# Recurrent part of a graph network: tile sums in two PSUM banks, a third of the second half's n gate computed ahead, last half's gates in PSUM

## The reference, cut to what matters

```python
def step(h, _):
    messages = h[col] @ W_msg.T + b_msg
    agg = jax.ops.segment_sum(messages, row, num_segments=num_nodes)   # 50000 nodes; row is src, col is dst
    gi = agg @ W_ih.T + b_ih
    gh = h @ W_hh.T + b_hh
    r = sigmoid(i_r + h_r);  z = sigmoid(i_z + h_z)
    n = tanh(i_n + r * h_n)
    return (1 - z) * n + z * h
```

## Time and profile before

| | |
|---|---|
| median of 3 runs | 5896.12 us |
| the profiled execution's own time | 5895.16 us |
| its span in the trace | 5893.1 us |
| PE busy | 3913.6 us (66%) |
| DVE busy | 3931.6 us (67%) |
| POOL busy | 3402.2 us (58%) |
| ACT busy | 2444.6 us (41%) |
| mean granted TensorE clock | 0.835 |
| tile sums, first L1678 to last L1783 start, steps 0 to 4 | 3081.2 to 3334.5, 3644.5 to 3899.1, 4211.7 to 4466.3, 4779.6 to 5035.1, 5349.1 to 5592.6 us |

### The profile page before, as it was taken

How to read it: one execution, slowest core, us unless ns; L and a number is a source line. 1 busy time by engine, 2 the same in 40 slices (tenths; PEclk the granted TensorE clock), 3 DMA queues, 4 the chain that set the end, 5 groups by cost and what they waited for, 6 DMA issues and landing times. The chain is left out here.

```text
span 5893.1 us, 58110 instructions
## 1 busy us (share of the span) xinstructions
PE 3913.6 (66%) x14140; PEld 2165.5 (37%) x14140; DVE 3931.6 (67%) x7616; ACT 2444.6 (41%) x4625; POOL 3402.2 (58%) x3399
## 2 busy tenths in 40 slices
PE   6754447401444830006889999999999988994498
PEld 4422223200222310004655555555555544553343
DVE  7876663587666268866777766866776677662276
ACT  6852222212222211104657545754574457443333
POOL 7747776775777537777547302720371047567777
PEclk9977668755666875558999999999999999996599
DMA  5643226774111777755866534643564356663144
GB/s 184 228 153 102 96 96 225 254 254 167 46 46 46 252 238 206 206 151 180 259 223 201 161 130 154 202 148 130 163 203 137 132 172 203 194 218 92 50 140 122
DMA packets 574298, 967.14 MB, mean 164 GB/s; under 512 B 98376, under 2 KB 250846, under 8 KB 573964
## 3 DMA queue, kind: packets, MB, share of 16 engines
q1 hardware_dynamic: 459308, 748.64, 39.2%
q0 software_dynamic: 100544, 163.41, 10.3%
q10 hardware_dynamic: 14112, 51.39, 2.2%
HBM read 530.33 MB, written 438.34 MB: 164 GB/s over the span
## 5 line engine op out<-in xcount | busy, mean ns | idle before, releaser
L1604 POOL DMA_INDIRECT r_G<-msg_tab,srow x980 | 927.0, 946 | 1273.4 <-DMA msg_tab<-r_m 959.0
L830 PE MATMUL cv_psO<-cv_V,cv_cwi 128*128 128x448 f32 x896 | 478.6, 702 | 857.4 <-DVEq L816 857.4
L830 PEld LDWEIGHTS cv_psO<-cv_V,cv_cwi 128*128 128x128 f32 x896 | 220.7, 254 | 1115.3 <-issue 595.5
L1150 POOL DMA_INDIRECT x_tab<-a_r,node_pos x392 | 380.8, 971 | 237.8 <-DVE a_r L1110 120.4
L1678 PE MATMUL r_psS<-r_sel,r_G 128*128 128x129 f32 x1960 | 326.5, 317 | 277.5 <-DMA r_G<-msg_tab,srow 158.7
L1783 DVE TENSOR_TENSOR agg<-r_psS,agg 128x129 f32 x980 | 283.6, 289 | 324.2 <-PE r_psS L1678 247.3
L696 POOL DMA_INDIRECT o_tab<-cv_ob,put_idx x392 | 388.7, 992 | 142.2 <-issue 115.6
L1647 PE MATMUL r_psHN<-r_hin,whh 128*128 128x512 f32 x882 | 457.5, 601 | 9.6 <-DMA r_hin<-ht_tab 9.4
L1652 PE MATMUL r_psR<-r_hin,whh 128*128 128x512 f32 x882 | 453.1, 595 | 0.0
L688 POOL DMA_INDIRECT cv_M<-h_tab,gat_src x392 | 374.5, 955 | 119.5 <-issue 119.5
L1636 PEld LDWEIGHTS r_psM<-wmsg,r_hnew 128*128 128x128 f32 x2744 | 348.2, 191 | 218.4 <-DVE r_hnew L1836 124.2
(11 more groups left out here) (260 smaller groups left out, 9895.8 us busy)
## 6 DMA issues: line engine op xcount, KB each, us to landing
r_hin<-ht_tab SPq DMA_DIRECT2D x441, 256.0 KB
msg_tab<-r_m SPq DMA_DIRECT2D x392, 256.0 KB
ht_tab<-r_hnew SPq DMA_DIRECT2D x343, 256.0 KB
o_tab<-o_blank SPq DMA_DIRECT2D x98, 512.0 KB, 4.5
st_h<-h_tab SPq DMA_DIRECT2D x98, 512.0 KB
st_o<-o_tab SPq DMA_DIRECT2D x98, 512.0 KB
i_x<-x_tab SPq DMA_DIRECT2D x49, 528.0 KB
r_x<-x_tab SPq DMA_DIRECT2D x98, 264.0 KB, 2.9
```

What stands on the lines that cost most here:

```text
L830: ins = nc.tensor.matmul(psO[:, h, 0:HW], cwi[m][:], V[i % 2][m][:, HW * h:HW * (h + 1)], start=m == 0, stop=m == 3)
L1150: pool.indirect_dma_start(x2_tab, bass.IndirectOffsetOnAxis(ap=node_pos[:, j:j + 1], axis=0), rb[i % RR][:, t, :], None).then_inc(s_out[i ...
L1604: pool.indirect_dma_start(G[g % GR][:, q, :], None, msg_tab[s % 3], bass.IndirectOffsetOnAxis(ap=srow[:, j:j + 1], axis=0)).then_inc(s_g[g ...
```

## The change

Tile sums: the four products of a group now fill one bank (128 columns each, not 129), and the groups alternate between the two banks, so PE waits for the adds of g-2 (`s_ev >= TQ * (g - 1)`). PE does group i-1 in turn i, ScalarE selects group i, VectorE adds group i-2. VectorE's turn becomes d1, add, d2, add, hnew, m, add, add, t1; in half 1 m of job i-2 comes before d1 of job i-1. The first z of half 1 is multiplied before the last group.

HN ahead: in turns i = 1, 4, ..., 46 of half 0 (16 of them) SyncE loads the state of a chunk c = i // 3 of half 1, PE multiplies it by whh's n columns into r_psR at the end of its turn, ScalarE adds the bias into SBUF after its select, and SyncE stores it to a new table. In half 1 these 16 chunks load it (r_kin) and have no HN; their t1 is a product of two SBUF tensors. R of the next job waits until ScalarE has emptied r_psR. In the last step this is done for all 49 chunks.

Last half: n and t2 are in r_psHN, z in r_psZ or the first tile bank by turns, not in SBUF.

```diff
-SW = P + 1
+SW = P
...
+        AHEAD = [(s, i, i // 3) for s in range(FIN1) for i in range(1, HALF, 3)] + [(FIN1, i, i) for i in range(HALF)]
+        ahead_at = {(s, i): a for a, (s, i, _) in enumerate(AHEAD)}
+        ahead_of = {(s, c): a for a, (s, _, c) in enumerate(AHEAD)}
+        ahead_n = [sum(1 for t, _, _ in AHEAD if t <= s) for s in range(STEPS)]
...
+        def kept(k):
+            s, h, i = JOBS[k]
+            return bool(h) and (s, i) in ahead_of
...
+            oin = [sb(f"r_oin{i}", [P, CW], F32, c6) for i in range(2)]
+            ohn = [sb(f"r_ohn{i}", [P, CW], F32, c6) for i in range(2)]
+            kin = [sb(f"r_kin{i}", [P, CW], F32, c6) for i in range(2)]
...
-            psS = [pb(f"r_psS{i}", [P, 2, 256], F32, c6) for i in range(2)]
+            psS = [pb(f"r_psS{i}", [P, TQ, SW], F32, c6) for i in range(2)]
...
-                return psI if h == 0 and i % 2 else psZ
+                if h and s == FIN1:
+                    return psS[0][:].rearrange("p q w -> p (q w)") if i % 2 else psZ[:]
+                return psI[:] if h == 0 and i % 2 else psZ[:]
+
+            def n_bank(k):
+                s, h, i = JOBS[k]
+                return ns[k % 2] if h and s < FIN1 else psHN[k % 2]
+
+            def t_sum(k):
+                return psHN[k % 2] if JOBS[k][0] == FIN1 else ts[k % 2]
+
+            def z_bank(k):
+                s, h, i = JOBS[k]
+                return zs[k % 2][:] if h and s < FIN1 else gate_bank(k)
...
+                def load_ahead(a):
+                    s, _, c = AHEAD[a]
+                    if s:
+                        b = job(s - 1, 1, c)
+                        sp.wait_ge(s_hst[b % 2], 16 * hst_n[b])
+                    if a >= 2:
+                        sp.wait_ge(s_op, a - 1)
+                    sp.dma_start(oin[a % 2][:], htv[HALF + c]).then_inc(s_oin[a % 2], 16)
+
+                def store_ahead(a):
+                    sp.wait_ge(s_oe, a + 1)
+                    sp.dma_start(hnv[AHEAD[a][2]], ohn[a % 2][:]).then_inc(s_ost[a % 2], 16)
+
+                def load_kept(k):
+                    s, h, i = JOBS[k]
+                    a = ahead_of[s, i]
+                    sp.wait_ge(s_ost[a % 2], 16 * (a // 2 + 1))
+                    if k >= 2:
+                        sp.wait_ge(s_t1, k - 1)
+                    sp.dma_start(kin[k % 2][:], hnv[i]).then_inc(s_kin[k % 2], 16)
...
+                    if turn and s == FIN1:
+                        for j in range(HALF + 1):
+                            if j == 0:
+                                load_ahead(ahead_at[s, 0])
+                                load_ahead(ahead_at[s, 1])
+                            elif j + 1 < HALF:
+                                load_ahead(ahead_at[s, j + 1])
+                            if j:
+                                store_ahead(ahead_at[s, j - 1])
+                        load_kept(k)
+                        load_kept(k + 1)
                     sp.wait_ge(s_d1, k + 1)
                     if k + 2 < len(JOBS):
                         load(k + 2)
+                        if kept(k + 2) and (JOBS[k + 2][0] < FIN1 or JOBS[k + 2][2] >= 2):
+                            load_kept(k + 2)
+                    if h == 0:
+                        if i == 0:
+                            load_ahead(ahead_at[s, 1])
+                        if (s, i - 1) in ahead_at:
+                            store_ahead(ahead_at[s, i - 1])
+                        if (s, i + 2) in ahead_at:
+                            load_ahead(ahead_at[s, i + 2])
...
+                def ahead(s, i):
+
+                    a = ahead_at[s, i]
+                    pe.wait_ge(s_oin[a % 2], 16 * (a // 2 + 1))
+                    pe.wait_ge(s_r, job(s, 0, i) + 1 if s < FIN1 else job(s, 1, 0))
+                    if a:
+                        pe.wait_ge(s_oe, a)
+                    nc.tensor.matmul(psR[:], whh[:, 2 * D:3 * D], oin[a % 2][:], start=True, stop=True
+                                     ).then_inc(s_op, 1)
+
+                def r_free(k):
+                    s, h, i = JOBS[k]
+                    if k:
+                        pe.wait_ge(s_r, k)
+                    if not h and (s, i - 1) in ahead_at:
+                        pe.wait_ge(s_oe, ahead_at[s, i - 1] + 1)
+                    if h and i == 0:
+                        pe.wait_ge(s_oe, ahead_n[s])
...
                     pe.wait_ge(s_sb, g + 1)
-                    if g:
-                        pe.wait_ge(s_ev, TQ * g)
+                    if g >= 2:
+                        pe.wait_ge(s_ev, TQ * (g - 1))
                     for q in range(TQ):
-                        nc.tensor.matmul(psS[q // 2][:, q % 2, 0:SW], G[g % GR][:, q, :], sel[g % 2][:, q, :],
+                        nc.tensor.matmul(psS[g % 2][:, q, :], G[g % GR][:, q, :], sel[g % 2][:, q, :],
                                          start=True, stop=True).then_inc(s_sel, 1)
...
-                            if k:
-                                pe.wait_ge(s_r, k)
-                            state_part(k, 0, psR)
+                            r_free(k)
+                            state_part(k, 0, psR[:])
                             bank_free(k)
                             state_part(k, 1, gate_bank(k))
                             if k:
                                 finish(k - 1)
                         elif i == 0:
                             finish(job(s - 1, 1, HALF - 1))
-                        if i >= 2:
-                            tiles(HALF * s + i - 2)
+                        if i:
+                            tiles(HALF * s + i - 1)
+                        if (s, i) in ahead_at:
+                            ahead(s, i)
                     for i in range(HALF):
                         k = job(s, 1, i)
+                        z = gate_bank(k)
+                        if kept(k):
+                            pe.wait_ge(s_hin[k % 2], 16 * (k // 2 + 1))
+                        else:
+                            hidden(k)
+                        r_free(k)
+                        state_part(k, 0, psR[:])
                         if i == 0:
-                            tiles(HALF * s + HALF - 2)
-                        hidden(k)
-                        pe.wait_ge(s_r, k)
-                        state_part(k, 0, psR)
-                        if i == 0:
+                            bank_free(k)
+                            state_part(k, 1, z)
                             tiles(HALF * s + HALF - 1)
                             pe.wait_ge(s_ev, EC * (s + 1))
-                        edge_part(k, 0, psR)
-                        bank_free(k)
-                        state_part(k, 1, psZ)
-                        edge_part(k, 1, psZ)
+                            edge_part(k, 0, psR[:])
+                        else:
+                            edge_part(k, 0, psR[:])
+                            bank_free(k)
+                            state_part(k, 1, z)
+                        edge_part(k, 1, z)
...
+                        select(HALF * s + i)
+                        if (s, i) in ahead_at:
+                            a = ahead_at[s, i]
+                            act.wait_ge(s_op, a + 1)
+                            if a >= 2:
+                                act.wait_ge(s_ost[a % 2], 16 * (a // 2))
+                            nc.scalar.activation(ohn[a % 2][:], psR[:], ACT.Identity, bias=bhh[:, 2:3]).then_inc(s_oe, 1)
...
-                        nc.scalar.activation(ns[k % 2][:], ts[k % 2][:], ACT.Tanh, bias=bih[:, 2:3]).then_inc(s_n, 1)
+                        nc.scalar.activation(n_bank(k)[:], t_sum(k)[:], ACT.Tanh, bias=bih[:, 2:3]).then_inc(s_n, 1)
...
+                    t = ts[k % 2]
                     if k >= 2:
                         dve.wait_ge(s_n, k - 1)
-                    nc.vector.scalar_tensor_tensor(ts[k % 2][:], psHN[k % 2][:], bhh[:, 2:3], rs[k % 2][:],
-                                                   ALU.add, ALU.mult).then_inc(s_t1, 1)
+                    if kept(k):
+                        nc.vector.tensor_tensor(t[:], kin[k % 2][:], rs[k % 2][:], ALU.mult).then_inc(s_t1, 1)
+                    else:
+                        nc.vector.scalar_tensor_tensor(t[:], psHN[k % 2][:], bhh[:, 2:3], rs[k % 2][:],
+                                                       ALU.add, ALU.mult).then_inc(s_t1, 1)
                     dve.wait_ge(s_pi, HALF * s + i + 1)
                     dve.wait_ge(s_t1, k + 1)
-                    nc.vector.tensor_tensor(ts[k % 2][:], ts[k % 2][:], psI[:], ALU.add).then_inc(s_t2, 1)
+                    if s == FIN1:
+                        dve.wait_ge(s_h, k - 1)
+                    nc.vector.tensor_tensor(t_sum(k)[:], t[:], psI[:], ALU.add).then_inc(s_t2, 1)
...
-                        g = HALF * s + i - 3
-                        at = ranks(g) if i >= 3 else None
-                        if i == 3 and s:
+                        g = HALF * s + i - 2
```

(58 more changed lines are left out.)

23 lines of the change are left out of this document (15 added, 8 removed).

## The result

The kernel after takes 5828.84 us (median of 4 runs, 5827.17 to 5829.56), the kernel before 5895.56 us beside it: ratio 0.9887, 95% interval 0.9870 to 0.9904. The forecast was 5816, with 5795 to 5828 as its own range, so the time lies inside the stated range and just over the forecast's own, 5 us under rival (b)'s 5834. Medians are of all runs of a kernel, ratios of the fast runs of both. The profiled execution took 5829.56 us, its span is 5827.5 us.

A forecast was written before the change was run, and what follows sets the result against it. PE bounds half 1, a 5.26 us loop through the adds half 0, PE and GpSimd the last half. Savings 40.2 (steps 1 to 3) + 16.8 (step 0) + 23.5 (step 4) = 80.5 give 5816 us; range 5764 to 5868.

The forecast's parts named there:

- rival (b): Last half: the scatters keep 1.403 us apart, 18 us less gain, 5834 us; chance 0.15.
- Half 0: Half 0: ordinary turns 4.97 us, ahead turns 5.93, 5.28 on average; plus 1.2 us a step in steps 1 to 3.
- the gain of the banks: Half 0: alternating banks end the wait on the adds, turn from 5.26 to about 5.0, 0.29 us a turn.
- the ahead path: Half 0: each of sixteen ahead turns costs 0.96 us through r_psR and ScalarE, 0.31 a turn on average.
- Rival (a): Half 0 runs at the gathers' pace, ScalarE's way through the ahead product hidden; 52 us less, 5764; chance 0.14.
- Half 1: Half 1: 15 jobs without HN save 15 x 0.86 = 12.9 us a step; PE keeps the lead.
- lead-in: Start of half 1: Z done before the first edges' low-clock products takes 1.7 us off, 0.9 in step 0.
- The sum of steps 0 to 3: Steps 1 to 3 save 13.4 us each, 40.2 together; step 0 saves 16.8.
- Step 4: Last step: half 0 costs nothing, GpSimd alone bounds the last half; saves 23.5 us, from 5.5 to 28.
- The scatters: Last half: 196 scatters come 1.31 us apart instead of 1.403, half a stretched one a turn; saves 18 us.
- The first scatter: Last half: first scatter 5.5 us earlier, from m of job 0 (2.9), one Z (1.7) and one HN (0.9).
- Rival (d): Half 0: PE's clock falls in every ahead turn, 166 us slower, 5982 us; chance 0.07.

The follow-up runs named there:

- e6: Kernel after without the ahead products of steps 0 to 3, run on a second chip; 5823.4 us, ratio 0.9891 to the kernel before.
- e11: e7 with PE's ahead product moved before M and tiles; 5762.1 us, ratio 0.9787 to the kernel before.
- e1: Kernel after with ScalarE emptying r_psR before its select in half 0 of steps 0 to 3; 6488.4 us, ratio 0.9946, on the slow chip.
- e9: Kernel after, unchanged, measured again on a third chip; 5819.1 us, ratio 0.9883 to the kernel before.
- e3: Kernel after with n, z and t2 of the last half back in SBUF; 6425.0 us, ratio 0.9886, on the slow chip.
- e4: Kernel after with r of the last half in PSUM too; 6429.1 us, ratio 0.9903, on the slow chip.
- e7: Kernel after with r_psR emptied before the select, last half's r in PSUM, its first two jobs' x rows loaded early; 5795.6 us, ratio 0.9843.
- e8: e7 with ahead products in two turns of three, 32 a step; 5766.3 us, ratio 0.9790 to the kernel before.
- e10: Kernel after with only last-half changes: r in PSUM, first two jobs' x rows loaded early; 5813.1 us, ratio 0.9873.
- e12: e11 with 32 ahead products a step instead of 16; 5733.8 us, ratio 0.9738 to the kernel before.
- e2: Kernel after without the ahead products of steps 0 to 3; 6534.5 us, ratio 1.0057, on the slow chip.

## Why the prediction was right, and where a term was off

**Half 0: right to a few hundredths.** 4.97 and 5.93 were forecast, 4.97 and 5.94 measured, and the pace stayed at 5.3. The ends were less exact: the adds ended 2.0, 2.2 and 0.6 us later than before in steps 1 to 3 (forecast 1.2 each) and 1.5 earlier in step 0 (forecast 3). That the gain of the banks was there and was taken back by the ahead path is shown by e6 (without the products 4.96 in every turn) and by e11 (with them, but without the chain, 5.05 and 4.97). The VectorE and ScalarE loop of 4.97 is the floor of half 0 in all of these, a hair under the gathers' 5.0.

**Rival (a), the gathers' pace,** was ruled out for this kernel for the right reason: a chain, not a load. e11 is the case it described. But the way there had two chains in it, not one, and the prediction (and e1's expectation) had seen only the first.

**Half 1: right, with luck in its lead-in.** 12.88 for 15 products of 0.858, no wait for the two further loads. The lead-in gave more in steps 1 and 2 (3.4 and 2.6 us, forecast 1.7) and 0.9 in step 3. Before, the products after the adds ran at the low clock in step 1 (granted 0.53 from 3899 to 3905 us) and for the most part in step 2, and at full speed in steps 0 and 3; after, they ran at full speed in all four, in this profile:

```profile
3887.16 1.12 PE L1760 MATMUL r_psR<-agg,wih 128*128 128x512 f32 x2 [2.11 <-DVE agg L1896]
3888.12 1.02 PE L1760 MATMUL r_psZ<-agg,wih 128*128 128x512 f32 x2
```

PE waits as long (2.11, before 1.96). The waits ahead of it don't decide it either. In step 3 the kernel after has waits of 0.58, 1.19 and 2.06 there, and its products start 0.96 and 0.86 apart; e9, the same kernel with the same three waits, runs at the low clock in the same place (0.96, then 1.66 and 1.71, and a lead-in 1.7 longer):

```profile
4988.58 1.13 PE L1760 MATMUL r_psR<-agg,wih 128*128 128x512 f32 x2 [2.06 <-DVE agg L1896]
4989.54 1.86 PE L1760 MATMUL r_psZ<-agg,wih 128*128 128x512 f32 x2
4991.20 1.91 PE L1822 MATMUL r_psI<-agg,wih 128*128 128x512 f32 x2
```

So after this wait the clock falls in some executions and not in others, 1.7 us a time, and the runs don't show what decides. Step 3's first 16 jobs of half 1 took 84.96, and before 96.23, less than in the other steps; why is open.

**The sum of steps 0 to 3 (56.7, forecast 57.0) is closer than its terms.** Half 0 came out 2.7 us worse than forecast over the four steps, the first 16 jobs of half 1 gave 1.7 less (49.9, forecast 51.6), the lead-in 1.7 more (7.7, forecast 6.0), and from the last hnew to the next step's first gather another 2.4 went that no term had. That they cancel is luck.

**Step 4: the mis-sized term,** 10.6 in place of 23.5. Two parts.

The scatters: I took one stretched scatter in two turns at 0.2 us, from the long ones of the earlier trace rows. The mechanism was right (e3, e4), the size was not. The stretch depends on how the two instructions meet: 0.24 at the most in the last half before, where all 92 that met one came 0.33 us or later into it, and 0.46 to 0.51 where one starts just behind t1's start. The scatters of step 3 in the kernel before, which the prediction left out, already reached 1.45. The stretched time adds up to 9.2 us in the kernel after, above 0.982 each, and 18.8 in the kernel before, so half of it was left where I had left a quarter. The pace was 1.350, not 1.31. e4's kind of change takes the rest, down to 1.302 to 1.308 (e7, e8, e10 to e12), not to the 1.29 that I took for a scatter without any stretch.

The first scatter: forecast 5.5 us earlier, measured not at all. The m of job 0 came out from behind the update as foreseen, but it then waited 2.26 for its x rows. The clock was low for all three products behind the adds (1.87, 1.71, 1.71 apart; before, the first of four was at full speed: 0.97, 1.42, 1.70, 1.15), so that R of job 1 starts 5.29 after the first of them, where HN before started 5.24 after it, though one product less lies between. And the last group's tiles came 4.7 us after the last gather's start, before 3.2 ([idle 2.31 <- DMA]), with the ahead store and the two kept loads issued 0.3 and 0.7 us after it. Whether these transfers are the cause isn't shown: in e9, the same kernel, the tiles came 3.5 after it, and its first scatter 263.9 us after the first gather, 2.1 less than before.

**On the page weighed in the prediction.** The runs contradict what the Trainium skill (SBUF — State Buffer, Who interferes with whom) infers, that an operation with two SBUF inputs doesn't hold up the generation of descriptors: scatters issued into such operations take up to 1.50 us and without them 0.98, on every chip here. The same section's rule that such an operation contends with GpSimd's reads would fit, if the issue of a scatter reads its row numbers from SBUF; no run here parts reads from writes. Its rule that an operation with at most one SBUF input doesn't contend with GpSimd agrees with all scatters here (at most 1.02 us).

**Rival (d)** (the clock falls in every ahead turn) didn't come: the granted clock of half 0 stayed 0.99. PE's idle time before R was 0.74 us by the profile, not 1.7: M waits for m (the psM bank) in each turn, so PE runs later than my sum had it, with the same slack shared out otherwise.

## What to carry to other kernels

Where a wait is removed from an in-order loop, sum the next loop instruction by instruction from distances between starts: three engines within 0.3 us of one another were told apart here that way, and a product that fits PE's time can still cost a whole chain when its bank is emptied behind another engine's long instruction. Put a guest product where its bank's owner has just been served (e11), and its emptying ahead of whatever is long and not urgent. Give each VectorE operation that runs beside GpSimd's indirect DMA issue at most one SBUF input, and leave none over. What one that is left costs depends on where the issues fall in it, and that moves when the rest of the turn is changed: fewer scatters were stretched after, but by up to 0.51 us instead of 0.24. Read all instructions of a kind before sizing a term, not those of one half. And before a wait or a late landing is put down to a change, compare the same place in every run that shares the change, and in a second profile of the same kernel.

## What the runs showed of the hardware that was not expected

An indirect scatter issued 0.05 to 0.54 us into a VectorE operation with two SBUF inputs (128x512, 0.68 to 0.75 us) ends 1.54 to 1.59 us after that operation's start, so it takes 1.02 to 1.50 us; issued at any other time, but for the operation's first 0.05 us, it takes 0.98 to 1.02. After a wait of 2.06 us PE's granted clock fell in one execution and stayed in another of the same kernel, at the same place. Chips differ: on one the same program took 6495 us where on others it took 5889 to 5896, its gathers spread over 292 us instead of 246 though each was issued in the same 0.94 us; half 0 ran at 6.0 us a turn there with or without ahead products, and these were then a gain, since half 1 kept its own (16 jobs took 83.82 us in e1 and 96.69 in e2; ratios 0.9946 and 1.0057, while the runs of the kernel before spread over 174 us on that chip).
